# Layer 0's moments on 128x2 numbers move from VectorE to GpSimd, and a maximum with zero becomes a Relu on ScalarE

## The reference, cut to what matters

```python
def _masked_instance_norm(x, mask):
    x = x * m
    n_valid = jnp.sum(m, axis=-1, keepdims=True)
    mean = jnp.sum(x, axis=-1, keepdims=True) / n_valid
    var = jnp.sum(x * x, axis=-1, keepdims=True) / n_valid - mean * mean
    x = (x - mean) / jnp.sqrt(jax.nn.relu(var) + EPS)
    return x * m
attn = softmax(q k / 4)
mean = jnp.einsum('bhqk,bhkd->bhqd', attn, v)
ex2 = jnp.einsum('bhqk,bhkd->bhqd', attn, v * v)
std = jnp.sqrt(jax.nn.relu(ex2 - mean * mean))
out = (xn * std + mean) * mask
```

## Time and profile before

| what | value |
|---|---|
| median of 3 runs | 3317.26 us (3314.8 to 3321.52) |
| the profiled execution's own time | 3316.17 us |
| its span | 3314.4 us, mean granted TensorE clock 0.922 |
| PE busy | 2816.2 us (85%) |
| DVE busy | 1860.3 us (56%) |
| ACT busy | 1329.2 us (40%) |
| POOL busy | 872.1 us (26%) |

### The profile page before, as it was taken

The page is one execution under the profiler, slowest core; times in us unless marked ns, Lnnn a source line. Parts: engine busy times, 40 slices in busy tenths (PEclk is TensorE's granted clock), DMA queues, the critical chain, the costliest instruction groups (busy, mean ns, idle before and its releaser), DMA issues. The chain is left out here.

```text
span 3314.4 us, 41358 instructions
## 1 busy us (share of the span) xinstructions
PE 2816.2 (85%) x14624; PEld 1319.0 (40%) x14624; DVE 1860.3 (56%) x4546; ACT 1329.2 (40%) x2326; POOL 872.1 (26%) x690
## 2 busy tenths in 40 slices
PE   4888888867999999998999999986568888888895
PEld 1222222214555555556656555542222333233332
DVE  3777777733334444301455655566867776667641
ACT  0555555552333333222333233422215544454562
POOL 1566666661344444420000010101111010100000
PEclk7999999988999999799999999987779899999897
DMA  4444444321002101213223232323333232323210
GB/s 98 96 96 96 99 99 98 81 64 60 21 27 71 38 27 34 71 39 83 53 60 61 63 69 55 67 61 84 75 82 86 69 77 57 89 55 74 65 34 20
DMA packets 182335, 219.92 MB, mean 66 GB/s; under 512 B 40841, under 2 KB 135665, under 8 KB 175985
## 3 DMA queue, kind: packets, MB, share of 16 engines
q1 hardware_dynamic: 170064, 189.74, 24.9%
q0 software_dynamic: 6016, 20.98, 1.9%
q10 hardware_dynamic: 6048, 6.56, 0.6%
HBM read 146.90 MB, written 51.64 MB: 60 GB/s over the span
## 5 line engine op out<-in xcount | busy, mean ns | idle before, releaser
L1259 DVE TENSOR_REDUCE l_M<-PS 128x1 f32<-128x512 f32 x512 | 329.4, 680 | 170.1 <-PE PS L722 169.7
L1485 DVE TENSOR_REDUCE l_M<-PS 128x1 f32<-128x512 f32 x512 | 334.7, 683 | 142.2 <-PE PS L967 138.8
L1198 ACT ACTIVATE l_P<-PS 128x512 f32<-128x512 f32 x512 | 286.7, 598 | 255.7 <-PE PS L977 237.7
L1558 POOL TENSOR_TENSOR l_S<-l_P 128x512 f32<-128x512 f32 x256 | 325.6, 1305 | 58.4 <-ACT l_P L1050 58.4
L1050 ACT ACTIVATE l_P<-PS 128x512 f32<-128x512 f32 x512 | 276.0, 598 | 136.6 <-PE PS L731 134.5
L967 PE MATMUL PS<-l_KS,l_QS 97*128 97x512 bf16 x512 | 205.2, 411 | 103.8 <-DVE l_M L1485 72.4
L1324 DVE TENSOR_REDUCE l1a_M<-PS 128x1 f32<-128x512 f32 x256 | 158.8, 681 | 206.3 <-PE PS L784 206.3
L722 PE MATMUL PS<-l_KS,l_QS 97*128 97x512 bf16 x512 | 202.0, 404 | 81.7 <-DVE l_M L1259 41.9
L1163 ACT ACTIVATE l_P<-l_P 128x1024 f32<-128x1024 f32 x128 | 135.2, 1057 | 299.5 <-DVE l_P L1405 299.1
L1391 DVE CUSTOM_DVE_ANT_0 l_JK<-PS,l_MK 128x256 f32<-128x256 f32 x512 | 195.8, 419 | 101.0 <-PE PS L897 98.8
L612 PE MATMUL PS<-l_YT,l_w_mlp_w 128*128 128x256 f32 x1024 | 235.9, 387 | 5.0 <-ACT l_YT L1125 4.9
(11 more groups left out here) (244 smaller groups left out, 4769.7 us busy)
## 6 DMA issues: line engine op xcount, KB each, us to landing
l_QS<-q_scratch SPq DMA_DIRECT2D x128, 128.0 KB, 5.6
q_scratch<-l_T SPq DMA_DIRECT2D x96, 128.0 KB
l_QS<-q_scratch SPq DMA_DIRECT2D x32, 384.0 KB, 4.9
k_scratch<-l_T SPq DMA_DIRECT2D x96, 128.0 KB
l_KS<-k_scratch SPq DMA_DIRECT2D x32, 384.0 KB
l_QS<-q_scratch SPq DMA_DIRECT2D x32, 256.0 KB, 5.6
l_KS<-k_scratch SPq DMA_DIRECT2D x32, 256.0 KB
l_RB<-l_recs SPq DMA_DIRECT2D x32, 256.0 KB
```

The lines of the kernel that those rows point to most:

```text
L1198: e.activation(t.P[quad % 4][:, m, :], PS[:, COUNTS.bank[st], :], ACT.Exp, scale=0.25).then_inc(q.sem("act.exp", st), 1)
L1259: e.tensor_reduce(t.M[i % 2][:, qt, hd:hd + 1], PS[:, COUNTS.bank[st], :], AX.X, ALU.max).then_inc(q.sem("dve.smax", st), 1)
L1485: e.tensor_reduce(t.M[i % 2][:, qt, hd:hd + 1], PS[:, COUNTS.bank[st], :], AX.X, ALU.max).then_inc(q.sem("dve.smax", st), 1)
L1558: x = e.tensor_tensor(t.S[j % 2][:, m, :], t.P[2 * j % 4][:, m, :], t.P[(2 * j + 1) % 4][:, m, :], ALU.add)
```

## The change: what it does

Four of the six small instructions of `0.f2` move from DVE to POOL, in a new `0.f2` step there (place 0.28 + 0.02). The reciprocal of the count moves into the end of `0.f1` on DVE. The last reciprocal stays on DVE, but its place moves from 0.28 to 0.28 + 0.3, and it now waits for POOL. The maximum with zero at the end of `0.f3b` (128x512, DVE) goes, and a Relu over the same tile is put on ACT directly ahead of each Sqrt, with a wait between the two. The two new waits on `act.sqrt` and `dve.f4` of the batch before keep POOL from overwriting columns of `sm` that are still read.

```diff
+         ("0.f2", "pool"): 0.02, ("0.f2", "dve"): 0.3,          # in LATER
-    "0.f2": ["dve.f2"],
+    "0.f2": ["pool.f2", "dve.f2"],
 # scalar0, "0.sq"
+                q.next_needs(e.activation(t.EX[b % 2][:, j, :], t.EX[b % 2][:, j, :], ACT.Relu))
                 e.activation(t.EX[b % 2][:, j, :], t.EX[b % 2][:, j, :], ACT.Sqrt, scale=t.sm[:, 14 + j:15 + j]
                              ).then_inc(q.sem("act.sqrt", st), 1)
 # vector0, "0.f1", j == 1
-                    e.tensor_reduce(sm[:, 4:5], MK[:, :], AX.X, ALU.add).then_inc(q.sem("dve.cnt", st), 1)
+                    q.next_needs(e.tensor_reduce(sm[:, 4:5], MK[:, :], AX.X, ALU.add))
+                    e.reciprocal(sm[:, 5:6], sm[:, 4:5]).then_inc(q.sem("dve.cnt", st), 1)
 # vector0, "0.f2"
-                q.wait_ge("dve.cnt", step("0.f1", i, 1))
-                q.next_needs(e.reciprocal(sm[:, 5:6], sm[:, 4:5]))
-                q.wait_ge("act.f1", step("0.f1", i, 1))
-                q.next_needs(e.tensor_scalar(sm[:, 6:10], sm[:, 0:4], sm[:, 5:6], None, ALU.mult))
-                q.next_needs(e.tensor_tensor(sm[:, 10:12], sm[:, 6:8], sm[:, 6:8], ALU.mult))
-                q.next_needs(e.tensor_tensor(sm[:, 12:14], sm[:, 8:10], sm[:, 10:12], ALU.subtract))
-                q.next_needs(e.tensor_scalar(sm[:, 12:14], sm[:, 12:14], 0.0, 1e-5, ALU.max, ALU.add))
+                q.wait_ge("pool.f2", st)
                 e.reciprocal(sm[:, 14:16], sm[:, 12:14]).then_inc(q.sem("dve.f2", st), 1)
 # vector0, "0.f3b"
-                q.next_needs(e.tensor_tensor(EX[:, j, :], EX[:, j, :], o[:, j, :], ALU.subtract))
-                e.tensor_scalar(EX[:, j, :], EX[:, j, :], 0.0, None, ALU.max).then_inc(q.sem("dve.f3b", st), 1)
+                e.tensor_tensor(EX[:, j, :], EX[:, j, :], o[:, j, :], ALU.subtract).then_inc(q.sem("dve.f3b", st), 1)
 # gpsimd0, new
+            elif kind == "0.f2":
+                sm = t.sm
+                q.wait_ge("act.sqrt", step("0.sq", i - 2, 1))
+                q.wait_ge("dve.f4", step("0.f4", i - 2, 1))
+                q.wait_ge("dve.cnt", step("0.f1", i, 1))
+                q.wait_ge("act.f1", step("0.f1", i, 1))
+                q.next_needs(e.tensor_scalar(sm[:, 6:10], sm[:, 0:4], sm[:, 5:6], None, ALU.mult))
+                q.next_needs(e.tensor_tensor(sm[:, 10:12], sm[:, 6:8], sm[:, 6:8], ALU.mult))
+                q.next_needs(e.tensor_tensor(sm[:, 12:14], sm[:, 8:10], sm[:, 10:12], ALU.subtract))
+                e.tensor_scalar(sm[:, 12:14], sm[:, 12:14], 0.0, 1e-5, ALU.max, ALU.add).then_inc(q.sem("pool.f2", st), 1)
```

More of the change, by code:

```diff
@@ L247 @@
     "0.fold": ["pool.fold"], "0.sums": ["pe.sums"], "0.sout": ["act.sums"],
-    "0.inv": ["dve.inv"], "0.f1": ["dve.f1", "act.f1"], "0.f11": ["dve.cnt"], "0.f2": ["dve.f2"],
+    "0.inv": ["dve.inv"], "0.f1": ["dve.f1", "act.f1"], "0.f11": ["dve.cnt"], "0.f2": ["pool.f2", "dve.f2"],
     "0.f3": ["dve.f3", "pool.f3", "act.f3y"], "0.f3b": ["dve.f3b"], "0.sq": ["act.sqrt"], "0.f4": ["dve.f4"], "0.f5": ["pool.f5"],
```

## The result

The changed kernel takes 3300.74 us in the median of four runs (3297.55 to 3307.88), the kernel before 3317.72 us on the same chip (3314.8 to 3321.52): a ratio of 0.9947, 95% interval [0.9926, 0.9967]. Two later sets of the same kernel on other chips gave 0.9927 [0.991, 0.9944] and 0.994 [0.9926, 0.9954]. It is faster, by 17 to 22 us between the medians, and not by the 39 us that were forecast. The profiled execution took 3297.55 us.

What follows compares the result with a forecast made beforehand. PE sets layer 0's pace, except where another engine stops it. 3316.17 - 26.0 (stops) - 16.1 (clock) + 1.4 (reciprocal) + 1.5 (Relu for maximum) = 3277.0 us, 3278 as median; range 3268 to 3297.

Steps and rivals of the forecast that it cites:

- Part 1, the stretch itself: Moving `0.f2` off DVE ends PE's stops there: 26.0 us of stops, 16.1 us of clock, less 1.4 us for the reciprocal.
- What is late next? ... Both are there: After the stop at `0.f2`, the POOL step and banks PE needs next are ready, so nothing new stops it.
- the clock term of 16.1 us: Low clock after the stops at `0.f2` in seven batches vanishes with them: 3 x 1.57 + 3 x 2.86 + 2.8 us.
- Part 3: Maximum at `0.f3b` becomes a Relu on ACT: about 0 in six batches, +1.3 us in the seventh, +0.2 in the eighth.
- The net of nothing: For six batches, Relu cost of 1.36 us against 1.29 saved at `0.f3b`: 0.1 us each, taken as 0.
- Table loads: Rival: Relu needs another ACT table, up to three more loads a batch at the square roots, 27 us, 3305; chance 0.06.
- Slow POOL instructions: Rival: the four small instructions on POOL take 3 us each, giving 3335; chance 0.07, shared with another new stop.
- Clock stays low: Rival: PE's stops at `0.f2` go, but the clock still falls there after other small stops, about 3294; chance 0.15.
- More at `0.f3b`: Rival: dropping the two maxima saves more than the Relus cost, 1.3 us more in six batches, 3270; chance 0.10.
- A new stop: Rival: another new stop, place not named, eats all the gain; chance 0.07, shared with slow POOL instructions.
- its own signs of being wrong: POOL additions ACT waits for, more table loads, low clock without a stop, or PE stopping on something else in freed time.
- arrives at the end whole: Barriers separate layer 0 from the rest, so its saving reaches the program's end whole; layer 1 starts some 39 us earlier.

Runs made afterwards that it cites:

- e5: The changed kernel, unaltered, run again on another chip: 0.9927 of the kernel before.
- e18: The changed kernel, unaltered, run once more on another chip: 0.994 of the kernel before.
- e9: Changed kernel with the moments' stores as four DMAs of 32 partitions per half instead of eight of 16, rows landing wrongly: 3277.2 us, 0.9896 of the kernel before.
- e10: Kernel before with the same halved stores of the moments, as a control: 0.9996 of the kernel before.
- e13: Changed kernel with ACT issuing the four second-moment stores of each half, SyncE keeping the other four: 0.9916 of the kernel before.
- e16: Changed kernel with ACT issuing four second-moment stores in only two of four halves per batch, items 0 to 12: 0.992 of the kernel before.
- e17: Same store relief as e16, but with the maximum left on DVE and no Relu: 3280.39 us, 0.9904 of the kernel before.
- e3: Changed kernel without the Relu, the maximum with zero left out altogether: 0.9903 of the kernel before.
- e2: Kernel before with only the maximum replaced by a Relu on ACT, `0.f2` still on DVE: 0.9998 of the kernel before.
- e1: Changed kernel with the maximum back on DVE and no Relu, the four small instructions still on POOL: 0.992 of the kernel before.
- e15: e1 run again, on the same chip as e13: 0.9943 of the kernel before.
- e4: Kernel before with DVE's `0.f2` moved from place 0.28 to 0.21, when POOL is idle: 0.996 of the kernel before.

## Why the prediction was right in most steps and wrong in its sum

- **Part 1, the stretch itself: right, but 40.0 is the best of three.** Stops and clock of the seven places, less the reciprocal, were put at 40.7 us; the matched matmuls give 40.0 in the first trace, and 35.1 and 34.0 in the other two, where the clock fell in two stretches more (e5, e18). The reciprocal costs what was put: the stop in front of it all grew from 1.00 to 1.21 us. POOL's instructions were put at 0.8 us and are 0.92; nobody waits for the additions behind them.
- **"What is late next? ... Both are there": the step that failed.** It looked at what PE needs inside the stretch, and there it was right. It didn't ask what PE's stop had been good for, and so it put the cost at the 0.f3 stretches at nothing; it is 16.9 us there (13.2 and 11.9 in the other two traces). SyncE has few pauses in the item but for its own transfers, and the stop of 3.76 us was its slack; with it gone RB comes 1 to 4 us late in the first trace, 23 to 25 us further on, and the turned maxima right behind it. PE's stops for these two grew from 0.60 to 2.73 us a batch there, 12.8 us in six (and by 6.5 us in e18); the rest of the growth is matmuls at the low clock. The Relu's part of the same stretches went the forecast way: the stops for DVE fell by 2.62 us a batch, that for ACT grew by 2.01. Taking half SyncE's store instructions away (e9) takes 16 us of these stretches back; doing it before (e10) gives nothing. That lateness in SyncE's queue makes these stretches longer is shown, not argued; e13 and e16 show it with every transfer made. In the whole program's time only e17 stands clear of the changed kernel on one chip. e9 has no changed kernel beside it on its chip; its interval meets that of the first set and overlaps e5's. That e9 is 37.6 us faster than the kernel before on its chip, near the 39 forecast, is in part luck: 5.0 us of it come from the end of layer 0 (92.9 us instead of 97.9), which the halved stores shorten in the kernel before too (e10, 94.2).
- **Part 1, the clock term of 16.1 us: about right at its place, but not a net gain.** In the first trace low clock at `0.f2` falls by 32 us of time and at `0.f3` rises by 20; over layer 0 it is 75.1, 89.0 and 95.6 us in three traces of the changed kernel, 85.5 in that of the kernel before. Where it falls varies from execution to execution at the same stops (e18's rows). So on average the low level is about as long as in the one trace of the kernel before. With SyncE relieved it is 64.9 to 71.7 us, 14 to 21 us less than before, where all 35.8 us at the seven places were to go. Whether the spread of the three sets (0.9927 to 0.9947) comes from the clock is not shown.
- **Part 3: right.** ACT's block at the square roots was to grow by 1.36 us; from the first Relu to the exponentials it is 286.99 - 281.74 = 5.25 us where it was 3.94, 1.31 more:

```profile
281.74 0.63 ACT L1071 ACTIVATE l_EX<-l_EX 128x512 f32<-128x512 f32 x1
282.39 1.28 ACT L1072 ACT_TABLE_LOAD   x1
...
284.31 0.61 ACT L1071 ACTIVATE l_EX<-l_EX 128x512 f32<-128x512 f32 x1
...
286.99 2.64 ACT L1050 ACTIVATE l_P<-PS 128x512 f32<-128x512 f32 x5
```

  PE's stop there is 3.67 us on average, 0.7 more than "about 3". Of the two stops for DVE ahead of it one fell from 2.14 to 0.46 us and the other from 0.94 to 0; what PE no longer waits there it waits here (without any Relu, e3's stop is 2.39 us, also 0.7 above the 1.66 of before). The net of nothing is borne out by e2 against the kernel before (0.9998). In the changed kernel, too, with and without Relu (e18, e5, after: 0.994, 0.9927, 0.9947; e1, e15: 0.992, 0.9943) no difference can be told; with SyncE relieved, e17 (without) is 6.8 us below e16 (with), at overlapping intervals.
- **The rivals.** Table loads: no more than before, eight at the square roots and seven back. The Trainium skill ("ScalarE: Activation LUTs", section "Table sets: the hidden batching unit") says relu is in every set, and the trace now agrees: 46 loads in the whole program, as before. Slow POOL instructions: none above 0.31 us. Clock stays low: in part at `0.f2` (two of six stretches in e5 and in e18) and in sum, see above; its time, 3294, is near the measured one, but mostly by another cause. More at `0.f3b`: not seen, e2 is at 0.9998. A new stop was given some chance, but only one that eats everything; that SyncE's queue would take the stop's place was among none of the rivals, and the range ended at 3297. Of its own signs of being wrong, the clock that is low and PE stopping on something else in the freed time came true.
- **Barriers: "arrives at the end whole": open.** In the first pair of traces layer 1 starts 27.6 us earlier and the program ends 18.6 us earlier. The spread of the later layers, 22.7 us over all traces, is too large to test it.

The Trainium skill ("Perfetto Trace Analysis", section "DMA Optimizations") says that balancing DMAs over the engines that can issue them may help when descriptor generation is what limits. e13 agrees as to SyncE (RB's load nearly on time again, 21.6 to 22.3 us after the 0.f2 stretch), and its ACT row shows the other side: an engine that computes pays 0.6 us for each.

## What to carry to other kernels

A stop of the busiest engine is also slack for every in-order queue beside it: before counting it as a gain, look at which queue has no other pause, and follow its issues to the next transfer that somebody waits for. Here the sign was in the trace of before: 39 issues of 0.6 us per item, and the longest gap between the 0.f2 stretch and RB's load that isn't a wait for a transfer of its own (2.8 us) stands at PE's stop. And when a stop with a low clock behind it goes, the clock's part is less certain than the stop's while other stops remain: of 30.9 us at the low clock in the six 0.f2 stretches 27.5 went in one trace, 16.9 and 13.8 in the two others.

## What the runs showed of the hardware

- Small DVE instructions on two numbers per partition: 0.16 us with POOL idle, 1.18 us beside POOL's two-input additions (e4 against the earlier trace rows); the four on POOL 0.19 to 0.31 us, never longer, with row maxima (PSUM in) on DVE beside them.
- TensorE's clock fell to 1.2 GHz after stops of only 1.21, 0.33 and 0.33 us in some executions of a stretch and not in others (15.6 against 12.6 us for the same 50 matmuls; e18 and the first trace).
- The switch to the other table and back costs 1.28 us each and no more: the square root starts 0.02 us after its load ends, and the load 0.02 us after the instruction before it (changed kernel, second batch).
- A DMA issue holds the issuing engine's queue for about 0.6 us, SyncE's as well as ACT's (e13: four issues, 2.44 us on ACT, its exponentials 2.57 us later).
